# Norms, residual and transposes behind attention, one batch at a time between the last units' steps

## The reference, cut to what matters

```python
x = x + _layernorm(_L0_attn_ref(_layernorm(x), ...))      # gated delta rule, 16 key heads, 32 value heads
x = x + _layernorm(_L0_ffn_ref(_layernorm(x), ...))       # router, top 6 of 32 experts, 2 shared experts
```

## Time and profile before

| what | value |
|---|---|
| time, median of 3 runs | 1457.39 us (1455.38 to 1457.75) |
| the profiled execution's own time | 1462.19 us |
| its span in the profile | 1459.8 us |
| PE busy in the span | 1314.2 us (90%) |
| DVE busy | 1078.9 us (74%) |
| ACT busy | 975.6 us (67%) |
| POOL busy | 665.2 us (46%) |
| mean granted clock of PE | 0.971 |

### The profile page before, as it was taken

The page is one execution under the profiler, slowest core; times in us unless marked ns, Lnnn a source line. Parts: engine busy times, 40 slices in busy tenths (PEclk is TensorE's granted clock), DMA queues, the critical chain, the costliest instruction groups (busy, mean ns, idle before and its releaser), DMA issues.

```text
span 1459.8 us, 33841 instructions
## 1 busy us (share of the span) xinstructions
PE 1314.2 (90%) x11516; PEld 912.9 (63%) x11516; DVE 1078.9 (74%) x2142; ACT 975.6 (67%) x2122; POOL 665.2 (46%) x726
## 2 busy tenths in 40 slices
PE   2679999999999999999999999999987469999995
PEld 2246676766666666766666666667666336666663
DVE  4577978879797979788797979788765445555555
ACT  2569788887989798888989797988865122222221
POOL 0125554546455454545464455545463306555550
PEclk9999999999999999999999999999999659999998
DMA  2111010101010110101010110100010024455441
GB/s 83 44 37 47 29 37 24 38 23 45 16 45 24 47 43 23 38 23 41 20 45 16 45 45 31 38 23 16 23 41 9 1 71 166 150 151 153 151 153 36
DMA packets 44656, 76.34 MB, mean 52 GB/s; under 512 B 7172, under 2 KB 26022, under 8 KB 44488
## 3 DMA queue, kind: packets, MB, share of 16 engines
q1 hardware_dynamic: 44488, 74.19, 16.3%
HBM read 72.85 MB, written 1.32 MB: 51 GB/s over the span
## 4 chain that ended last, share of the span: by engine, by line
PE 68%; DVE 18%; issue 6%; ACT 6%; DVEq 1%; DMA 0%; SPq 0%; POOL 0%; ACTq 0%; POOLq 0%
PE bank L561 12%; PE bank L779 8%; DVE sil L1132 7%; PE products L732 6%; PE products L709 5%; PE bank L515 4%; PE products L515 4%; PE bank L617 3%; PE products L605 3%; PE products L723 3%; PE bank L637 3%; DVE t L1189 3%; PE bank L645 3%; PE products L712 2%; PE bank L580 2%
## 5 line engine op out<-in xcount | busy, mean ns | idle before, releaser
L561 PE MATMUL bank<-xT,whl 128*128 128x512 f16 x1152 | 305.7, 382 | 13.4 <-DVE sil L1132 9.3
L1378 POOL TENSOR_TENSOR hsq<-hsq,qsq 128x512 f32<-128x512 f32 x64 | 81.4, 1273 | 483.5 <-ACT hsq L982 483.5
L1132 DVE SCALAR_TENSOR_TENSOR sil<-bank,cw,sil 128x510 f32<-128x510 f32 (+2 forms) x384 | 283.2, 737 | 9.7 <-ACT sil L854 4.3
L1189 DVE CAST_PREDICATED t<-levm,bank 128x256 f16<-128x256 uint8 x384 | 165.5, 431 | 114.1 <-PE bank L637 57.0
L1021 ACT ACTIVATE kq<-vtok 128x512 f16<-128x512 f32 x94 | 59.2, 630 | 192.1 <-DVE vtok L1309 192.1
L950 ACT ACTIVATE x<-bank 128x256 f16<-128x256 f32 x320 | 123.5, 386 | 94.6 <-PE bank L617 89.9
L1202 DVE CAST_PREDICATED u<-levm,bank 128x256 f16<-128x256 uint8 x384 | 162.9, 424 | 0.0
L561 PEld LDWEIGHTS bank<-xT,whl 128*128 128x128 f16 x1152 | 93.9, 98 | 85.6 <-DVE sil L1132 13.7
L779 PE MATMUL bank<-wmhl,kq 128*128 128x256 f16 x1128 | 138.4, 273 | 0.3
L617 PE MATMUL bank<-t,n 128*128 128x64 f16 x1536 | 109.6, 194 | 25.9 <-DVE t L1189 23.1
L617 PEld LDWEIGHTS bank<-t,n 128*128 128x128 f16 x1536 | 80.3, 98 | 83.6 <-DVE t L1189 61.7
(11 more groups left out here) (159 smaller groups left out, 3153.6 us busy)
## 6 DMA issues: line engine op xcount, KB each, us to landing
grow<-rowsc SPq DMA_DIRECT2D x64, 256.0 KB, 3.3
wt<-wqkvz SPq DMA_DIRECT2D x16, 768.0 KB, 4.5
wms<-wm SPq DMA_DIRECT2D x47, 256.0 KB, 4.1
zs<-gsc SPq DMA_DIRECT2D x18, 512.0 KB, 3.9
wo<-wout SPq DMA_DIRECT2D x16, 256.0 KB, 3.8
zs<-gsc SPq DMA_DIRECT2D x8, 448.0 KB, 3.8
zs<-gsc SPq DMA_DIRECT2D x8, 384.0 KB, 3.6
zs<-gsc SPq DMA_DIRECT2D x9, 320.0 KB, 3.6
```

What stands on the lines that cost most here:

```text
L561: mm = nc.tensor.matmul(dst[:, :], whl[:, h, k, col:col + HD], xT[:, l, k, half * 512:(half + 1) * 512], start=(k == 0 and m == 0), stop=( ...
L1132: nc.vector.scalar_tensor_tensor(out=dst[:, :, late:S], in0=src[:, :, 0:S - late], scalar=cw[:, q, i, 3 - late:4 - late], in1=dst[:, :, la ...
L1189: nc.vector.copy_predicated(halves(t16[:, pair(U)], n)[:, :, :, 0], by4(2 * n, n), packed(X_BANK, n)).then_inc(s_tup, 1)
```

## The change

The work behind attention is cut into eight pieces for each batch, in this order: `stats` (DVE: statistics of the attention's output), `rstd` 0 (ACT: logarithm and exponential), `normed` 0 (DVE: normalize, residual, statistics of the sum), `rstd` 1 (ACT), `normed` 1 (DVE: normalize into `xn`), `turn` (PE: four transposes into bank 0), `turned` (ACT: high part), `low` (DVE: low part). For k, the pieces' number, b = k // 2. `sequence()` keeps a list of pieces that are due; each `acc` of the last group puts its batch's eight in and takes one out, and each step named in `BETWEEN` takes one out, which then stands right behind that step. What is left when the slots end follows in order. Only DVE, ACT and PE get new steps; SP's and POOL's streams stay as they are.

```diff
+ENDED = (("stats", 0), ("rstd", 0), ("normed", 0), ("rstd", 1), ("normed", 1), ("turn", 0), ("turned", 0), ("low", 0))
+BETWEEN = (("t", 2), ("t", 4), ("u", 6), ("rr", 0), ("rr", 1), ("r1h", 0), ("hz", 0), ("ht", 0))
 def sequence():
...
+    ended = []
     for n in range(-2 * B, (HQK + 2) * B):
         for what, k, lag in SLOT:
...
             elif 0 <= n - lag < HQK * B:
                 yield what, k, unit(0, n - lag)
+                b = n - lag - (HQK - 1) * B
+                if what == "acc" and b >= 0:
+                    ended += [(part, 2 * b + i) for part, i in ENDED]
+                if ended and (what, k) in BETWEEN or what == "acc" and b >= 0:
+                    part, i = ended.pop(0)
+                    yield part, i, (None, HQK)
+    for part, i in ended:
+        yield part, i, (None, HQK)
...
+            def turn(_, k):
+                b = k // 2
+                pe.wait_ge(s_gd, GD_SCAL + (b + 1) * GD_BATCH)
+                wait_g(pe, s_empty, (None, HQK - 1), FILLS, FILLS)
+                if b:
+                    pe.wait_ge(s_tpl, 4 + b)
+                for kk_ in range(2):
+                    for t in range(2):
+                        mm = nc.tensor.transpose(FB[0][:, (2 * kk_ + t) * P:(2 * kk_ + t + 1) * P],
+                                                 xn[:, 2 * b + t, kk_ * P:(kk_ + 1) * P], ident)
+                mm.then_inc(s_tp, 1)
...
-            transpose_tokens(4, s_gd, GD_LN2)
...
+            def rstd_(_, k):
+                b, second = k // 2, k % 2
+                logs_and_exps()
+                act.wait_ge(s_gd, GD_SCAL + b * GD_BATCH + (11 if second else 4))
+                nc.scalar.activation(lnv[:, 2 * b:2 * b + 2], mv[:, 2 * b:2 * b + 2, 1], ACT.Ln, bias=bias[:, 0:1]
+                                     ).then_inc(s_lna, 1)
+                act.wait_ge(s_lna, 2 + 2 * k + 1)
+                nc.scalar.activation(rstd[:, 2 * b:2 * b + 2], lnv[:, 2 * b:2 * b + 2], ACT.Exp, scale=-0.5
+                                     ).then_inc(s_lna, 1)
+            def turned(_, k):
+                b = k // 2
+                act.wait_ge(s_tp, 4 + b + 1)
+                nc.scalar.mul(xT[:, 0, :, b * S:(b + 1) * S], FB[0][:, :].rearrange("p (k t) -> p k t", k=2), SPLIT
+                              ).then_inc(s_tpe, 1)
...
-            rsqrt_var(GD_ST2, 3)
-            rsqrt_var(GD_ST3, 5)
-            copy_transposed(4)
...
+            def batch_statistics(src, b):
+                for t in (2 * b, 2 * b + 1):
+                    step(nc.vector.bn_stats(stats[:, t], src[:, t]))
+                settle()
+                for t in (2 * b, 2 * b + 1):
+                    step(nc.vector.bn_aggr(mv[:, t], stats[:, t]))
+            def stats_(_, k):
+                dve.wait_ge(s_acc, 4 * (HQK - 1) + k // 2 + 1)
+                batch_statistics(acc, k // 2)
+            def normed(_, k):
+                b, second = k // 2, k % 2
+                both = slice(2 * b, 2 * b + 2)
+                src, dst = (xs, xn) if second else (acc, acc)
+                dve.wait_ge(s_lna, 2 + 2 * k + 2)
+                settle()
+                for t in (2 * b, 2 * b + 1):
+                    step(nc.vector.tensor_scalar(dst[:, t], src[:, t], mv[:, t, 0:1], rstd[:, t:t + 1],
+                                                 ALU.subtract, ALU.mult))
+                if not second:
+                    settle()
+                    step(nc.vector.tensor_tensor(xs[:, both], xs[:, both], acc[:, both], ALU.add))
+                    settle()
+                    batch_statistics(xs, b)
...
+            def low_turned(_, k):
+                b = k // 2
+                dve.wait_ge(s_tpe, 4 + b + 1)
+                nc.vector.scalar_tensor_tensor(out=xT[:, 1, :, b * S:(b + 1) * S],
+                                               in0=FB[0][:, :].rearrange("p (k t) -> p k t", k=2), scalar=SPLIT,
+                                               in1=xT[:, 0, :, b * S:(b + 1) * S], op0=ALU.mult, op1=ALU.subtract
+                                               ).then_inc(s_tpl, 1)
...
-            dve.wait_ge(s_acc, 4 * HQK)
-            statistics(acc, GD_ST2)
-            normalize(acc, acc, 4)
-            settle()
-            step(nc.vector.tensor_tensor(xs[:], xs[:], acc[:], ALU.add))
-            settle()
-            statistics(xs, GD_ST3)
-            normalize(xn, xs, 6)
```

More of the change, by code:

```diff
@@ L45 @@
 GD_ST1, GD_LN1, GD_ABS, GD_G, GD_BETA, GD_SCAL = 16, 24, 26, 29, 31, 33
-GD_ST2, GD_ST3, GD_LN2, GD_LMAX, GD_GATES, GD_ST4, GD_OUT = 49, 74, 82, 85, 107, 127, 136
+GD_BATCH = 13
+GD_LN2 = GD_SCAL + 4 * GD_BATCH
+GD_LMAX, GD_GATES, GD_ST4, GD_OUT = GD_LN2 + 3, GD_LN2 + 25, GD_LN2 + 45, GD_LN2 + 54
 GP_BIAS, GP_ZERO = 3, 5
@@ L734, in proj @@
                 mm.then_inc(s_op, 1)
-            attention({"fill": fill, "rest": rest, "kk": kk, "x": x, "w": w, "y0": y0_, "y1": y1_, "y2": y2_, "p": p,
+            def turn(_, k):
[9 more added lines that the diff above has]
+                mm.then_inc(s_tp, 1)
+            attention({"turn": turn, "fill": fill, "rest": rest, "kk": kk, "x": x, "w": w, "y0": y0_, "y1": y1_, "y2": y2_, "p": p,
                        "o": o, "ss": ss, "proj": proj})
-            transpose_tokens(4, s_gd, GD_LN2)
             pe.wait_ge(s_tpl, 8)
@@ L995, in inverse_root @@
                 nc.scalar.activation(hrs[:, pair(U)], hrs[:, pair(U)], ACT.Exp, scale=-0.5).then_inc(s_rr, 1)
-            attention({"evict": evict, "hi": high_weights, "silu": silu, "nexp": norm, "cap": cap, "exb": row_factors,
+            def rstd_(_, k):
[12 more added lines that the diff above has]
+                              ).then_inc(s_tpe, 1)
+            attention({"rstd": rstd_, "turned": turned, "evict": evict, "hi": high_weights, "silu": silu, "nexp": norm, "cap": cap, "exb": row_factors,
                        "exp": factors, "cross": cross_, "n16": high_n, "xe": xe, "g": guess, "vn": solved,
@@ L1024, in _ @@
                 high(n)
-            rsqrt_var(GD_ST4, 7)
+            rsqrt_var(GD_ST4, 19)
         @block.vector
@@ L1249, in acc_ @@
                                         KB_BANK[:, :], ALU.add).then_inc(s_acc, 1)
-            attention({"tap": tap, "lo": low_weights, "sc": scalars, "nmul": norm, "mask": mask, "nt": decayed, "t": t,
+            def batch_statistics(src, b):
[4 more added lines that the diff above has]
+                    step(nc.vector.bn_aggr(mv[:, t], stats[:, t]))
@@ new lines, in stats_ @@
+            def stats_(_, k):
[15 more added lines that the diff above has]
+                    batch_statistics(xs, b)
+                else:
+                    assert done[0] == GD_SCAL + (b + 1) * GD_BATCH
@@ new lines, in low_turned @@
+            def low_turned(_, k):
[5 more added lines that the diff above has]
+                                               ).then_inc(s_tpl, 1)
+            attention({"stats": stats_, "normed": normed, "low": low_turned, "tap": tap, "lo": low_weights, "sc": scalars, "nmul": norm, "mask": mask, "nt": decayed, "t": t,
@@ L1252, in _ @@
                        "u": u, "rr": residual, "r1h": right_side, "hz": hz_, "ht": ht_,
                        "acc": acc_})
-            dve.wait_ge(s_acc, 4 * HQK)
-            statistics(acc, GD_ST2)
-            normalize(acc, acc, 4)
-            settle()
-            step(nc.vector.tensor_tensor(xs[:], xs[:], acc[:], ALU.add))
-            settle()
-            statistics(xs, GD_ST3)
-            normalize(xn, xs, 6)
-            assert done[0] == GD_LN2
             dve.wait_ge(s_mconst, 64)
@@ L1266, in _ @@
             split_small(rws[:], 3, NE - NSH)
-            low_transposed(4)
             score = lg[:, :, NPAD:]
@@ L1328, in _ @@
             statistics(acc, GD_ST4)
-            normalize(acc, acc, 8)
+            normalize(acc, acc, 20)
             settle()
```

## The result

The change makes the kernel slower: 1466.01 us median (1464.25 to 1468.43, 5 runs) against 1456.15 us of before on the same chip (5 runs), a ratio of 1.0051 with a 95% interval of 1.0033 to 1.0068. That is 7.4 us by the ratio, 4.8 to 9.9 by its interval, where 4.3 was forecast; the two medians alone differ by 9.9, the interval's upper end. The profiled executions differ by 6.4 in their spans (1466.2 and 1459.8).

What follows compares the result with a forecast made beforehand. The prediction took DVE's chain as the bound behind attention, and PE, `xe` and `t` waits in the slots. -9.9 there, +12.7 in the slots and +1.5 for the clock gave +4.3: 1461.7 us median, range 1455.5 to 1466.5.

Steps and rivals of the forecast that it cites:

- The stretch behind attention: From the last `acc`'s end to the first router matmul: 11.8 us against 21.7, a gain of 9.9.
- Slot 62: Batch 0's statistics and `normed` 0 on DVE and ACT's waiting pairs delay the last `xe`: 4.7 us lost.
- Slot 63, first half: Batch 0's `normed` 1, `turn`, `turned` and `low` delay level 3's `t`: 2.4 us lost.
- The clock: PE's clock falls up to a slot earlier, catching one more `o` and small steps: 1.5 us, between 0 and 5.
- half clock through the last slots: Rival: both new PE holes bring the clock down, costing 5 us; sum +7.8, 1465.2 us, chance 0.15.
- Slot 63's second half and the slots 64 and 65: Batch 1's pieces ahead of the last `xe` cost 4.4 us; later pieces in slots 64 and 65 together 1.2.
- the 9.9 that decide: Sign: the change wins if batch 0's `acc` end to batch 3's grows by less than 9.9 us.
- the two queues that hold the chain: In slot 62, DVE's `normed` 0 delays `u` and ACT's waiting pairs delay the last `xe`, together 4.7 us.
- The pieces lie in idle time: Rival: DVE's 5.7 us idle in slot 62 takes the pieces, slots pay 5.0; 1452.5 us, chance 0.14.
- No change to be told: Rival: the clock costs nothing and small pieces are a tenth shorter; sum +1.8, 1459.2 us, chance 0.29.

Runs made afterwards that it cites:

- e1: The change with all 32 pieces moved behind the last `acc`, none left in the slots: 1471.75 us, ratio 1.0090 against the kernel before.
- e5: The change with its pieces moved out of slots 62 and 63 into later gaps where DVE, ACT and PE idle: 1447.85 us, ratio 0.9924 against the kernel before.
- e2: The change with ACT's `rstd` pairs in slots 62 and 63 issued later, where their input is long there: 1465.69 us, ratio 1.0047 against the kernel before.
- e4: e2 with `normed` 0 also moved behind level 6's `u` in slots 62 and 63: 1463.83 us, ratio 1.0031 against the kernel before.
- e3: The change with 35 matmuls into an unused bank filling PE's holes in slots 62 and 63: 1461.89 us, ratio 1.0029 against the kernel before.
- e7: The change with batch 0's `normed` 1, `turn`, `turned` and `low` moved out of slot 63's first half: 1460.60 us, ratio 1.0014 against the kernel before.
- e8: The kernel before with matmuls into an unused bank in PE's holes from slot 64 to the b2s matmuls: 1454.78 us, ratio 0.9973 against the kernel before.
- e9: e5 with matmuls into an unused bank added in PE's holes, in the slots and behind them: 1445.66 us, ratio 0.9904 against the kernel before.

## Why the prediction was right, and where its sizes were off

**The stretch behind attention.** 9.9 forecast, 10.4 measured. Nearly each row came out as taken: normalize 0.73, residual 0.69, `bn_stats` 0.74, ACT's pair with its hops 0.60; `bn_aggr` is 0.25 for 0.16. The 0.5 more than forecast is batch 2's transposes, which found full clock: 0.75 from the normalized tile to ACT's copy in place of 1.20. e1 (7.9 a batch) and e5 (8.1 left) rest on the same sum.

**Slot 62.** ACT's first wait, the copy at 1113.91, the second wait and the last `xe` at 1119.57 came as worked out; 4.3 in place of 4.7. e2 and e4 show both causes, from batch 0's `acc` to `o`: 8.67 in the change, 7.28 without ACT's waits, 4.93 with the piece off DVE's chain too, 4.30 before.

**Slot 63, first half.** "2.4" for `normed` 1, `turn`, `turned` and `low` was too little. From slot 62's `o` to level 3's `t` the distance grew from 7.99 to 13.14, by 5.2. In e3, where the clock stays at 1.00, it is 11.45: the pieces cost 3.5, the clock the other 1.7 (1.2 of them `o`, which the forecast has in its term for the clock). What the 2.4 lacks is the normalize at 2.04 in place of 0.73, 1.3 us. I took its length from a place where POOL was idle, and no row has DVE's normalize beside POOL. The trace of before had a hint, though, in an instruction that reads two tensors in SBUF: `ht` takes 0.89 while POOL's `nl` runs until 1123.57, and 0.69 with POOL idle, in DVE's timeline:

```profile
1123.23 0.89 DVE L1240 TENSOR_TENSOR hT<-hz,hrs 128x512 f32<-128x512 f32 x1
...
1138.31 0.69 DVE L1240 TENSOR_TENSOR hT<-hz,hrs 128x512 f32<-128x512 f32 x1
```

e7 takes the four pieces away and gets 4.2 back of the whole first distance.

**The clock.** This is the term of the sum that was sized wrong: 1.5 forecast, 4.3 by e3's profile, 3.2 by its ratio. It caught not one `o` and some small steps but also `p`, the transposes and `proj` (3.76 for 1.97). The rival "half clock through the last slots" had sized this term at 5, nearer to what came.

The direction was as forecast; what sets it off was not. The forecast has the clock fall in the holes of over 3 us, but it had fallen at 1116.14, ahead of the first of them, and at 1129.7, ahead of the second. What the first fall hangs on stays open: before, with the same steps a little closer together, kept 1.00 there. It also differs between executions of the same instructions: unit 62's `o` ran at half clock in before and e1, at full clock in e5 and e8, whose streams are the same up to there. The Trainium skill's rule (TensorE: Matmul & The Clock Gate, "HAM oscillation — how this bites in real kernels"), that waits between bursts bring the clock down, agrees in so far as e3, with the holes filled and no piece moved, has 1.00 in place of 0.72; the fall at 1116.14, behind waits of 0.54 us and less, is not one that its long waits explain. And the half clock of the earlier trace rows at 1130 has PE busy for 2.94 of 3.00 us, so that row by itself doesn't show a fall where PE grows sparse, as the prediction reads it.

**Slot 63's second half and the slots 64 and 65.** From batch 1's `acc` to `o` pass 8.50 in place of 3.95, which is 4.6 for 4.4. Behind it the clock favoured the change once (`proj` 1.99 for 3.62) and disfavoured it twice (unit 63's `o`, 1.2 us longer, and `ss` 2.07 for 1.41), which nearly cancels. So that the two stretches together (5.3) are near their 5.6 is in part luck; without the clock the slots 64 and 65 cost some 0.9 for the 1.2 forecast. `normed` 0 in slot 65 did cost nothing, though POOL beside it made it 3.7 us long for 2.4: it ended 0.6 ahead of ACT's release, and `ht` started 0.1 behind that.

**The sum.** Median against median the loss is 9.9 us, by the ratio 7.4, in the two profiles 6.4. e1 explains part of that spread: slots with the same instructions as before took 42.8 where the profiled execution of before took 45.3, so that execution was among the slower ones. The time of 1466.01 lies in the range, near its upper end; that the slots would grow by more than the 9.9 that decide was right (16.7). It lies above the 1460.3 to 1464 that the forecast gave itself, and beside the 1465.2 of the half clock: the direction, the two queues that hold the chain, and the pieces' part of the slots (12.5 by e3, 12.7 forecast) were right; the size missing is the clock's.

**The rivals.** "The pieces lie in idle time" fell at the places of this change: DVE's idle 5.7 us a slot didn't help. At other places, e5's, it is what happens, for most of the pieces. (The sum there takes 5.0 for a third of 12.7, which would be 4.2; nothing hangs on it.) "No change to be told" (1459.2) fell too, as the interval's lower end is 1.0033.

## What to carry to other kernels

Idle time of an engine is a place for more work only where nobody waits for what comes next on that engine: look in the timeline for the single gaps and what ends them, not at the busy share, and put the piece into a gap whose end doesn't depend on it. When a step is spread over several engines, place each engine's part by itself, a small instruction that must wait behind another engine's new one at a spot where its input is long there. A delay in a PE chain can be paid twice, here 12.5 us as the delay and 3 to 4 in the clock. A gap that was measured beside PE at half clock shrinks when PE runs at full clock, as e9's `acc` shows; and a gain ends where the next thing is late, here also the gates' DMAs.

## What the runs showed of the hardware that was not expected

- DVE's f32 normalize on SBUF (`tensor_scalar`, a pair of 128x256) takes 0.72 to 0.74 with POOL idle and 1.54 to 2.05 while POOL works on SBUF tensors (0.73 to 0.89 where POOL worked beside a part of it); an f32 add of two SBUF tensors 0.69 and 1.04 to 1.09. `bn_stats` pairs took 0.75 beside POOL as well. The Trainium skill (GPSIMD Engine Reference, "1. Specifications") names it: the two engines share their SBUF interfaces, with contention for DVE instructions in a 2-port performance mode or with two SBUF inputs. The trace agrees for the add, which reads two SBUF tensors, and has the sizes; whether the normalize runs in such a mode no run shows.
- Matmuls that compute nothing, put into PE's holes, made the change 4.1 us faster (median 1461.89 after 1466.01; 3.2 by the ratios, whose intervals overlap a little) and the kernel before 3.9.
- ACT's logarithm on 128x2 takes 0.29 and the exponential 0.20, as long as on 128x8 (0.30 and 0.21): cutting such a step in four makes it cost four times as much.
